# The norm product in two column tiles, its lower bound on the sums in PSUM, and the roots spread by transfers

## What is computed

```python
def l2norm(t):
    return t / jnp.maximum(jnp.linalg.norm(t, axis=-1, keepdims=True), 1e-12)

q = l2norm(q) * qs
k = l2norm(k) * ksc
q = q * cos * scale + rotate_half(q) * sin * scale
k = k * cos * inv + rotate_half(k) * sin * inv
out = local_attention(q, k, v)
```

## Time and profile before

| | |
|---|---|
| median of 3 executions | 1865.2 us (1863.66 to 1868.27) |
| the profiled execution | 1865.6 us, span 1863.8 us |
| TensorE busy | 1804.9 us, 97% |
| VectorE busy | 1531.7 us, 82% |
| ScalarE busy | 1455.7 us, 78% |
| GpSimd busy | 1359.5 us, 73% |
| granted clock of TensorE, mean | 0.998 |

### The profile page before, as it was taken

The page is one execution under the profiler, slowest core; times in us unless marked ns, Lnnn a source line. Parts: engine busy times, 40 slices in busy tenths (PEclk is TensorE's granted clock), DMA queues, the critical chain, the costliest instruction groups (busy, mean ns, idle before and its releaser), DMA issues.

```text
span 1863.8 us, 67159 instructions
## 1 busy us (share of the span) xinstructions
PE 1804.9 (97%) x26763; PEld 1367.6 (73%) x26763; DVE 1531.7 (82%) x3002; ACT 1455.7 (78%) x2976; POOL 1359.5 (73%) x1165
## 2 busy tenths in 40 slices
PE   6999998999999999999999999999999999999997
PEld 4777776777777777777777777777777777777774
DVE  5776777788889888888888888888888888888886
ACT  5766665688788878888887888878878888887884
POOL 3010033899889888888888898889888888888880
PEclk9999999999999999999999999999999999999999
DMA  3000001344444444444443444444444444444342
GB/s 111 1 1 0 0 25 38 96 123 115 101 101 115 106 112 104 100 112 103 119 110 97 104 111 111 115 107 101 105 110 109 114 99 107 112 103 100 95 106 64
DMA packets 188251, 170.91 MB, mean 92 GB/s; under 512 B 20112, under 2 KB 187192, under 8 KB 187960
## 3 DMA queue, kind: packets, MB, share of 16 engines
q1 hardware_dynamic: 187960, 166.84, 35.9%
HBM read 21.01 MB, written 1.05 MB: 12 GB/s over the span
## 4 chain that ended last, share of the span: by engine, by line
PE 65%; ACT 12%; DVE 11%; issue 7%; POOL 4%; DMA 0%; SPq 0%; ACTq 0%; POOLq 0%; DVEq 0%
PE bank L1010 6%; PE bank L1051 6%; PE bank L978 6%; PE pair_bank L1029 5%; PE bank L1061 4%; PE bank L1113 3%; PE bank L1062 3%; PE bank L1063 3%; PE bank L1039 3%; PE bank L1135 3%; PE bank L896 2%; ACT sq L655 2%; DVE rot_v L1377 2%; ACT probs L735 2%; DVE rot_u L1376 2%
## 5 line engine op out<-in xcount | busy, mean ns | idle before, releaser
L436 POOL TENSOR_TENSOR z_norm<-probs_t,z_raw 128x512 f32<-128x512 f32 x376 | 480.9, 1279 | 101.2 <-DVE probs_t L1458 101.2
L442 POOL TENSOR_TENSOR z_raw<-rot_u,rot_v 128x512 f32<-128x512 f32 x384 | 498.3, 1302 | 70.8 <-DVE rot_v L1377 69.6
L1376 DVE TENSOR_TENSOR rot_u<-bank,tabs 128x512 f32<-128x512 f32 x384 | 262.9, 685 | 175.9 <-ACT sq L655 174.5
L1061 PE MATMUL bank<-x_high,w_high 128*128 128x256 f32 x768 | 302.1, 393 | 0.0
L469 POOL TENSOR_TENSOR sqs<-sq 128x512 f32<-128x512 f32 x192 | 246.3, 1283 | 60.5 <-issue 59.3
L1377 DVE TENSOR_TENSOR rot_v<-bank,tabs 128x512 f32<-128x512 f32 x384 | 261.1, 680 | 0.0
L1051 PEld LDWEIGHTS bank<-probs_t,v_late 128*64 128x64 f32 x3072 | 155.0, 137 | 144.5 <-issue 144.5
L655 ACT ACTIVATE sq<-bank 128x512 f32<-128x512 f32 x384 | 222.1, 593 | 24.1 <-PE bank L1063 17.7
L731 ACT ACTIVATE pair_bank<-pair_bank 128x512 f32<-128x512 f32 x192 | 111.7, 582 | 165.0 <-DVE pair_bank L1357 163.4
L664 ACT ACTIVATE probs_t<-bank 64x512 f32<-64x512 f32 x340 | 200.8, 591 | 22.7 <-PE bank L1039 20.7
L1063 PE MATMUL bank<-x_low,w_high 128*128 128x256 f32 x768 | 216.3, 282 | 0.0
(11 more groups left out here) (190 smaller groups left out, 4533.9 us busy)
## 6 DMA issues: line engine op xcount, KB each, us to landing
zqk<-z_norm SPq DMA_DIRECT2D x768, 128.0 KB
v_late<-v_sb SPq DMA_DIRECT2D x192, 192.0 KB, 2.6
w_stage<-in_L_ffn_Wqkv SPq DMA_DIRECT2D x24, 384.0 KB, 3.6
v_late<-v_sb SPq DMA_DIRECT2D x192, 32.0 KB, 2.2
wo<-in_L_ffn_Wo SPq DMA_DIRECT2D x24, 128.0 KB, 2.4
w<-in_L_ffn_W SPq DMA_DIRECT2D x12, 170.5 KB, 2.7
z_norm<-in_L_attn_x SPq DMA_DIRECT2D x4, 256.0 KB, 5.0
out<-z_raw SPq DMA_DIRECT2D x4, 256.0 KB, 2.3
```

Source lines behind the costliest of these rows:

```text
L436: return pool.tensor_tensor(z_norm[:, parity, idx, :, :], rinv(m)[:, idx, :].unsqueeze(1).broadcast_to([P, 2, T]), z_raw[:, parity, idx, : ...
L442: pool.tensor_tensor(z_raw[:, parity, idx, :, :], rot_u[:, idx, :, :], rot_v[:, idx, ::-1, :], ALU.add).then_inc(S[mark], 1)
L1061: pe.matmul(dst, w_high[:, r, j, cols], x_high[:, odd, :], start=True, stop=False)
L1376: dve.tensor_tensor(rot_u[:, idx, :, :], src, tabs[:, 2 * idx, :, :], ALU.mult)
```

## The change

The matrix of blocks has 64 columns instead of 128, so that a head's sum stands in 16 rows. Two products of 256 columns take the place of one of 512: the sums of q go to rows 0 to 63 of B_N, those of k to rows 64 to 127, each in its half of the array's columns. B_N then holds 128x256.

The bound is taken before the logarithm, as a maximum on the sums in PSUM (1e-24, the square of the reference's 1e-12). It comes on VectorE right behind the rotation of k. Logarithm and root are 128x256.

Four transfers of SyncE spread the root to 128 rows for k and q (`wide`). The bound and the root of group s+3 are made in slot s as before; GpSimd now normalises group s+2 in slot s, one slot later, in place: z_raw and z_norm become one tile z with four groups. SyncE's queue now has the transfers of v_late first, then those of the roots, then those of z. GpSimd's sum of squares stays between the norms of k and of q.

```diff
-    put("blk", i // 32 == np.arange(P)[None, :] // 32)
+    put("blk", i // 32 == np.arange(P // 2)[None, :] // 16)
...
-        z_raw = sb("z_raw", [P, 2, 2, 2, T])
-        z_norm = sb("z_norm", [P, 2, 2, 2, T])
+        z = sb("z", [P, G, 2, 2, T])
...
+        def wide(m):
+
+            return (late_wide if m >= G else early_wide)[:, m % 2, :, :]
...
             def slot(s):
+                if active(s, -3, GROUPS - 3):
+
+                    g, odd = (s + 3) % G, (s + 3) // G % 2
+                    cols = slice(g * GW, (g + 1) * GW)
+                    sp.wait_ge(S["lv_ready"], s + 4)
+                    sp.dma_start(v_late[WIN:P, odd, :, cols], v_sb[0:P - WIN, odd, :, cols]).then_inc(S[f"v_late_in{g}"], 16)
+                    sp.dma_start(v_late[0:WIN, odd, 1, cols], v_sb[P - WIN:P, odd, 0, cols]).then_inc(S[f"v_late_in{g}"], 16)
+                    sp.wait_ge(S["rinv_ready"], s + 4)
+                    after(sp, "zn_ready", s + 2)
+                    for idx in range(2):
+                        for k in range(2):
+                            sp.dma_start(wide(s + 3)[k:P:2, idx, :], rinv(s + 3)[64 * idx:64 * idx + 64, :]).then_inc(S[f"wide_in{(s + 3) % 2}"], 16)
...
             def normalise(m, idx):
 
-                parity = m % 2
-                return pool.tensor_tensor(z_norm[:, parity, idx, :, :], rinv(m)[:, idx, :].unsqueeze(1).broadcast_to([P, 2, T]), z_raw[:, parity, idx, :, :], ALU.mult)
...
+                zs = z[:, m % G, idx, :, :]
+                return pool.tensor_tensor(zs, wide(m)[:, idx, :].unsqueeze(1).broadcast_to([P, 2, T]), zs, ALU.mult)
...
-                if two:
-
-                    pool.wait_ge(S["bound_ready"], s + 4)
-                    after(pool, f"z_in{(s + 1) % G}", 16 * HG * ((s + 1) // G + 1))
-                    pool.wait_ge(S["k_summed"], s + 4)
-                    normalise(s + 3, 1)
+                if near:
+                    pool.wait_ge(S[f"wide_in{s % 2}"], 16 * HG * ((s + 2) // 2 + 1))
+                    pool.wait_ge(S["k_summed"], s + 3)
+                    normalise(s + 2, 1)
...
-                    act.wait_ge(S["n_done"], m + 1)
-                    act.activation(ln_n(m), B_N[:, :].rearrange("p (a t) -> p a t", a=2), ACT.Ln, bias=tiny[:, 0:1], scale=LNS).then_inc(S["ln_done"], 1)
+                    act.wait_ge(S["bound_ready"], m + 1)
+                    after(act, f"wide_in{m % 2}", 16 * HG * (m // 2))
+                    act.activation(ln_n(m), B_N[:, 0:T], ACT.Ln, bias=tiny[:, 0:1], scale=LNS).then_inc(S["ln_done"], 1)
...
-                pe.matmul(B_N[:, :], con("blk"), sqs[:, :, :].rearrange("p a t -> p (a t)"), start=True, stop=True).then_inc(S["n_done"], 1)
+                for idx in range(2):
+                    rows = slice(64 * idx, 64 * idx + 64)
+                    mm = pe.matmul(B_N[rows, 0:T], con("blk"), sqs[:, idx, :], start=True, stop=True, tile_position=(0, 64 * idx), skip_group_check=True)
+                mm.then_inc(S["n_done"], 1)
...
+                if two:
+                    dve.wait_ge(S["n_done"], s + 4)
+                    dve.tensor_scalar(B_N[:, 0:T], B_N[:, 0:T], 1e-24, None, ALU.max).then_inc(S["bound_ready"], 1)
...
-                if two:
-                    dve.wait_ge(S["rinv_ready"], s + 4)
-                    dve.tensor_scalar(rinv(s + 3), rinv(s + 3), 1e12 / ROOT, None, ALU.min).then_inc(S["bound_ready"], 1)
```

More of the change, by code:

```diff
@@ L62 @@
 _at = 0
-for _name, _n in (("ident", P), ("mask_causal", P), ("mask_local", 4 * KEYS), ("blk", P),
+for _name, _n in (("ident", P), ("mask_causal", P), ("mask_local", 4 * KEYS), ("blk", P // 2),
                   ("center", P), ("avg", P), ("rot", 4 * T)):
@@ L364, in slot @@
                         for half in range(2):
-                            sp.dma_start(zqk[half:P:2, g, :, pair, :], z_norm[64 * pair:64 * pair + 64, s % 2, :, half, :]).then_inc(S[f"z_in{g}"], 16)
-                if active(s, -3, GROUPS - 3):
-                    g, odd = (s + 3) % G, (s + 3) // G % 2
-                    cols = slice(g * GW, (g + 1) * GW)
-                    sp.wait_ge(S["lv_ready"], s + 4)
-                    sp.dma_start(v_late[WIN:P, odd, :, cols], v_sb[0:P - WIN, odd, :, cols]).then_inc(S[f"v_late_in{g}"], 16)
-                    sp.dma_start(v_late[0:WIN, odd, 1, cols], v_sb[P - WIN:P, odd, 0, cols]).then_inc(S[f"v_late_in{g}"], 16)
+                            sp.dma_start(zqk[half:P:2, g, :, pair, :], z[64 * pair:64 * pair + 64, g, :, half, :]).then_inc(S[f"z_in{g}"], 16)
                 if 0 <= s < G:
@@ L433, in normalise, with rotated @@
             def normalise(m, idx):
-                parity = m % 2
-                return pool.tensor_tensor(z_norm[:, parity, idx, :, :], rinv(m)[:, idx, :].unsqueeze(1).broadcast_to([P, 2, T]), z_raw[:, parity, idx, :, :], ALU.mult)
-            def rotated(m, parity, idx, prod, mark):
+                zs = z[:, m % G, idx, :, :]
+                return pool.tensor_tensor(zs, wide(m)[:, idx, :].unsqueeze(1).broadcast_to([P, 2, T]), zs, ALU.mult)
+            def rotated(m, idx, prod, mark):
                 pool.wait_ge(S[prod], m + 1)
-                after(pool, "zn_ready", m - 1)
-                pool.tensor_tensor(z_raw[:, parity, idx, :, :], rot_u[:, idx, :, :], rot_v[:, idx, ::-1, :], ALU.add).then_inc(S[mark], 1)
+                after(pool, f"z_in{m % G}", 16 * HG * (m // G))
+                pool.tensor_tensor(z[:, m % G, idx, :, :], rot_u[:, idx, :, :], rot_v[:, idx, ::-1, :], ALU.add).then_inc(S[mark], 1)
             def split_input(unit, b, odd):
@@ L452, in slot @@
                 g = s % G
-                one, two = active(s, -4, GROUPS - 4), active(s, -3, GROUPS - 3)
+                one, near = active(s, -4, GROUPS - 4), active(s, -2, GROUPS - 2)
                 if s == 0:
@@ L469, in slot @@
                     pool.tensor_tensor(sqs[:, :, :], sq[:, :, 0, :], sq[:, :, 1, :], ALU.add).then_inc(S["sums_ready"], 1)
-                if two:
-                    pool.wait_ge(S["q_summed"], s + 4)
-                    normalise(s + 3, 0).then_inc(S["zn_ready"], 1)
+                if near:
+                    pool.wait_ge(S["q_summed"], s + 3)
+                    normalise(s + 2, 0).then_inc(S["zn_ready"], 1)
                 if one:
-                    rotated(s + 4, s % 2, 0, "q_prod", "q_summed")
+                    rotated(s + 4, 0, "q_prod", "q_summed")
                 if g == 0 and active(s, -4, GROUPS - 8):
```

19 lines of the change are left out of this document (10 added, 9 removed).

## The result

| | before | after |
|---|---|---|
| median | 1864.7 us (4 runs) | 1911.9 us (4 runs, 1910.3 to 1915.0) |
| ratio to before | | 1.0252, 95% interval 1.0232 to 1.0271 |
| span of the profiled execution | 1863.8 us | 1911.2 us |
| first scores of the stream | 332.0 us | 338.7 us |
| last scores of the stream | 1830.0 us | 1879.1 us |

The change makes the kernel 2.5% slower. The forecast was 1866 us with a range up to 1905, so the result lies outside it. In the two spans the difference is 47.4 us: 6.7 before the first scores, 42.4 between the first and the last window product (their starts are 1497.4 us apart before and 1539.8 after), and -1.7 behind the last.

What follows compares the result with a forecast made beforehand. TensorE sets the pace, with a VectorE-ScalarE ring less than 5% behind that takes over after the change. The terms +82 - 74 - 7 = +1 us gave 1866 us, range 1830 to 1905.

Steps and rivals of the forecast that it cites:

- The norm product: On TensorE, two products of 256 columns in place of one of 512: 0.86 becomes 0.48 us a slot, -73 us of work.
- The bound in the ring: VectorE's new maximum before ScalarE's logarithm: L1355 to L696 grows from 3.31 to 3.80 us in 168 slots, +82 us.
- the ring: VectorE and ScalarE handing work to each other: 7.54 us in a slot of 7.84, to become the pace, 70 in 100.
- The ring stops waiting for a TensorE that is ahead of it: VectorE's and ScalarE's waits for the norm product, projections and scores (41.9, 17.7, 14.7 us) go: -74 us.
- L1458 gone: VectorE's old minimum behind the weights goes; its excess beside GpSimd counts in about two slots of eight: -7 us.
- z one slot later: GpSimd's result reaches the scores by SyncE's transfer: 4.2 to 4.6 us needed, 4.3 available plus room; price 0.
- the second rival: z comes too late at SyncE's transfers, delaying the scores 0.5 us in half of the slots: +48, 1915 us; 15 in 100.
- TensorE stays the pace: Rival: VectorE and ScalarE have more room than one slot shows, so TensorE's 73 us are paid out: 1792 us; 15 in 100.
- Halves do not overlap: Rival: the two half products on TensorE gain nothing, it keeps 7.84 us a slot: about 1870 us; 3 in 100.
- Late z: z's transfer arrives after the scores need it, 0.5 us in half of the slots: +48, 1915 us; 15 in 100.

## Why the prediction was wrong, point by point

**The norm product (0.48 us, -73): right in size, and little of it could reach the end.** The prediction said "earned and not paid". Measured alone, on the kernel before, it pays 24 us.

**The bound in the ring (+0.49 us in seven of eight slots, +82): the size of the step was right, the number of slots was not.** It is 3.80 us from L1367 to L705 and 8.03 for the slot, as forecast, and nothing in 1-2 (+0.06), the slot behind the GELU. But the start of the step, 3.31 us, held in three slots of eight; in the others the distance already contained waits. The prediction charged the step in all of them and gave those waits back in the next term. Without the bound and with z early the kernel is 58.6 us faster, which includes the shorter L1415.

**"The ring stops waiting for a TensorE that is ahead of it: -74 us": the first of two steps that failed.** The prediction took one slot, 6-7, as the pattern of all, and then gave back every wait on TensorE in full. With z early (norm of q first), the table shows what is left: 63.7 - 62.7 = 1.0 us more per period. Full payment is 7 x 0.49 = 3.4, so 2.4 came back per period, 24 x 2.4 = 57 us, where the prediction had 74 and 7 more for L1458. The waits say much the same: in that kernel 3.6 us are left of the 17.7 at the squares, 7.7 of the 14.7 at the maximum, and 3.0 stand newly at the bound, 60 us less than before. The norm product's part of the 74 (41.9) went as a whole; the waits for scores and projections went only in part.

**Slot 0-1 isn't the ring.** 0.43 of the 1.0 us stand there, 24 x 0.43 = 10 us, in a slot that VectorE fills with its own work after the change. The prediction had no term for a VectorE instruction that becomes longer where it now stands. What L1415 beside GpSimd costs by itself no run shows: without the bound it is short again, and moved behind the weights it stays long.

**L1458 gone (-7): not seen.** VectorE's total stayed (1531.7 before, 1532.2 after). 48 instances of the layer norm's product grew by 1281 - 610 = 671 ns, 32 us together, while 188 x (562 - 423) = 26 us went with L1458: the time beside GpSimd moved from one instruction to another. The 7 us can't be told apart from the 57 above.

**z one slot later (price 0): the second step that failed, and it was the second rival.** "4.3 us plus some 0.9 of room" was read in one slot. TensorE waited for z in 83 slots, some 59 us, and the kernel with the norm of q first is 18.3 us faster. The mechanism is the named one, SyncE's wait ahead of z, but the delay comes from GpSimd's order as much as from the queue: z waits for a norm that waits for squares. The priced rival had 48 us, 0.5 us in half of the slots, all of it paid; it was 59 us of waits, of which 18 reached the end, since other limits covered the rest. The section that the prediction names for some 2.0 us of fixed cost (the Trainium skill, DMA: Bandwidth & Descriptors, Anatomy of one DMA) is about transfers that GpSimd issues. SyncE issues z's, and they landed after 2.5 us in the median; the 4.2 to 4.6 us were reckoned from rows and don't need it.

**The start.** 6.7 us before the first scores were in no term. In the three kernels without a bound and with the norm product as in the change the first scores come at 330.5 to 331.7 us, against 338.7. ScalarE waits 11.9 us for the bound in the four early slots. A part may be the clock: between 300 and 320 us TensorE was busy for 12.7 us, 15.5 before, and between 320 and 340 us the granted clock was 0.71, 0.91 before and 1.00 in those three kernels. The lower of the two levels (1.2 GHz in place of 2.4) stood three times before the first scores, once before. So the bound starts this, at a place that the prediction did not look at; how much is waiting and how much is the clock was not separated.

**The sum again.** +82 - 57 = 25 for the stream with z early, some 10 of them VectorE's own work in slot 0-1; 6 to 7 at the start; 18 for z: 49 against the 47 measured. The forecast had half of the mechanism (a TensorE saving that isn't paid in full, a bound in the ring that is), and missed by credits 24 us too large and by 24 us put at nothing. The rival "TensorE stays the pace" (1792) is refuted by the run on the kernel before, where 24 us of its 73 were paid. "Halves do not overlap" is refuted by the 0.48 us.

**The range.** Late z was priced on top of a ring of +1 (1915), and the ring's own range ended at 1890. The result is a miss in the ring, in the start and in z together, and the list of cases held them apart. That the late-z price of 1915 lies 3 us from the result is luck: of its 48 us for z 18 were paid, and the rest came from the ring and from the start.

## What to carry to other kernels

Where two engines hand work to each other beside a full one, measure the distance from one handover to the next in every phase of the period, not in one slot: a saving on the full engine is paid only in the phases that it bounds (24 of some 73 us here), and a longer ring is charged in full only where the ring had no wait in it (two phases of eight here). A wait that goes away is a credit only if what ends it really moves. And a guard (a clamp, a bound) belongs behind a result that is due late, not on the path of one that is due now; here the guard cost 58.6 us in one place and some 14 in another. An instruction that is moved also meets other company: the layer norm's product was not touched by the change and took twice as long after it.

## What the runs showed of the hardware

- VectorE's 128x256 minimum from SBUF to SBUF took 286 ns alone and 1138 in the mean of the stream, ending 0.15 to 0.19 us after GpSimd's instruction; with its source in PSUM and its result in SBUF it took 407 to 426 ns beside the same work.
- VectorE's product of two 128x256 tiles in SBUF (L1415) took 0.41 us alone and 1281 ns in the mean where GpSimd worked beside it in 46 of 48 instances.
- Four fp32 instructions of 256 columns in two halves of the columns take 0.48 us of TensorE's time to the start of the next product, two of 512 took 0.86.
- SyncE's queue issued ten small transfers without a pause in 6.53 us at 448.94 us of the kernel without a bound and with the norm of q first, and in 7.29 us at 902.95, where the last of the four root transfers took 1.38 us.
